# A graph-attention layer on one core: GpSimd normalises all four blocks of a group with the mean itself, and the steps around the first pass are reordered

## What is computed

```python
h = jnp.maximum(_layernorm(x, axis=-1), 0.0)      # mean and variance per row, eps 1e-5
Wh = h @ W
f1, f2 = Wh @ a[:128, 0], Wh @ a[128:, 0]
e = leaky_relu(f1[:, None] + f2[None, :], 0.2)
e = where(adj == 0, -inf, e)
out = x + softmax(e, axis=1) @ Wh
```

## Time and profile before

| | us |
|---|---|
| median of 3 runs | 812.27 |
| the runs | 810.42, 812.27, 812.67 |
| the profiled execution, its own time | 809.52 |
| its span in the trace | 807.8 |
| PE busy | 784.1 |
| DVE busy | 740.3 |
| ACT busy | 482.0 |
| POOL busy | 421.6 |

### The profile page before, as it was taken

The page is one execution under the profiler, slowest core; times in us unless marked ns, Lnnn a source line. Parts: engine busy times, 40 slices in busy tenths (PEclk is TensorE's granted clock), DMA queues, the critical chain, the costliest instruction groups (busy, mean ns, idle before and its releaser), DMA issues.

```text
span 807.8 us, 22596 instructions
## 1 busy us (share of the span) xinstructions
PE 784.1 (97%) x8971; PEld 718.4 (89%) x8971; DVE 740.3 (92%) x1191; ACT 482.0 (60%) x776; POOL 421.6 (52%) x621
## 2 busy tenths in 40 slices
PE   5789999999999999999999999999999999999997
PEld 4679899999999999999999999999999999999986
DVE  7898899999999999999999999999999999999996
ACT  5688855655655555565555556565555656555542
POOL 8778755544545454454545445554544545454320
PEclk9999999999999999999999999999999999999999
DMA  9999899999999999999999999999999999998200
GB/s 180 165 106 88 79 108 117 108 93 110 85 101 91 101 90 89 110 85 101 89 103 90 88 109 87 100 87 105 90 88 105 90 101 86 106 89 88 27 14 17
DMA packets 48069, 75.99 MB, mean 94 GB/s; under 512 B 4514, under 2 KB 13348, under 8 KB 48036
## 3 DMA queue, kind: packets, MB, share of 16 engines
q0 software_dynamic: 43008, 67.13, 88.4%
q1 hardware_dynamic: 4880, 8.39, 3.0%
q10 hardware_dynamic: 148, 0.07, 0.0%
HBM read 272.70 MB, written 4.19 MB: 343 GB/s over the span
## 4 chain that ended last, share of the span: by engine, by line
PE 91%; DMA 4%; DVE 3%; issue 1%; ACT 1%; POOL 0%; ACTq 0%; DVEq 0%; POOLq 0%
PE acc L404 54%; PE acc L408 28%; PE stage L394 7%; DMA masks<-in_adj_dram 2%; DVE wt_ring L847 2%; DMA xm<-in_x_dram 2%; PE stage L377 1%; PE stage L386 1%; PE stage L359 0%; DVE pairs L837 0%; POOL masks L225 0%; DVE stats L778 0%; ACT marks L598 0%; DVE xm L949 0%; ACT xn L548 0%
## 5 line engine op out<-in xcount | busy, mean ns | idle before, releaser
L847 DVE SCALAR_TENSOR_TENSOR wt_ring<-stage,packed,marks 128x512 f32<-128x512 f32 x1024 | 697.7, 744 | 52.3 <-PE acc L408 42.4
L404 PE MATMUL acc<-pairs,wt_ring 128*128 128x258 f16 x4096 | 719.8, 274 | 4.0 <-DVE pairs L837 2.8
L408 PE MATMUL acc<-pairs,wt_ring 128*128 128x129 f16 x4096 | 698.1, 219 | 0.0
L404 PEld LDWEIGHTS acc<-pairs,wt_ring 128*128 128x128 f16 x4096 | 396.2, 97 | 59.1 <-DVE pairs L837 4.5
L598 ACT ACTIVATE marks<-stage 128x1024 uint16<-128x1024 uint8 x256 | 262.1, 1024 | 290.2 <-PE stage L394 289.4
L408 PEld LDWEIGHTS acc<-pairs,wt_ring 128*128 128x128 f16 x4096 | 399.7, 98 | 2.5
L246 POOL TENSOR_TENSOR masks<-masks 128x256 int32<-128x256 int32 x256 | 184.4, 735 | 238.1 <-ACT masks L618 237.3
L219 POOL DMA_DIRECT2D masks<-in_adj_dram x240 | 130.3, 545 | 99.5 <-PE stage L394 77.4
L618 ACT ACTIVATE masks<-masks 128x512 uint16<-128x512 uint16 x256 | 158.9, 622 | 2.7 <-DMA masks<-in_adj_dram 2.7
L394 PE MATMUL stage<-ident,masks 128*128 128x128 f32 x512 | 98.9, 275 | 0.7 <-ACT marks L598 0.5
L394 PEld LDWEIGHTS stage<-ident,masks 128*128 128x128 f32 x512 | 53.0, 141 | 5.3 <-issue 1.7
(11 more groups left out here) (67 smaller groups left out, 144.5 us busy)
## 6 DMA issues: line engine op xcount, KB each, us to landing
masks<-in_adj_dram POOLq DMA_DIRECT2D x256, 256.0 KB, 7.3
out_dram<-xm SPq DMA_DIRECT2D x15, 256.0 KB, 7.2
xm<-in_x_dram SPq DMA_DIRECT2D x1, 1536.0 KB, 13.2
xm<-in_x_dram SPq DMA_DIRECT2D x2, 512.0 KB, 5.7
xm<-in_x_dram SPq DMA_DIRECT2D x1, 1024.0 KB, 10.1
xm<-in_x_dram SPq DMA_DIRECT2D x2, 256.0 KB, 3.0
out_dram<-xm SPq DMA_DIRECT2D x4, 64.0 KB, 2.3
wx<-in_L_gnn_W_dram ACTq DMA_DIRECT2D x1, 64.0 KB, 3.1
```

The lines of the kernel that those rows point to most:

```text
L404: return nc.tensor.matmul(acc[:, r, 0:2 * E1], wtv[:, w, r, 1, :], pairv[:, t, :, 0:E1], start=st, stop=end)
L408: return nc.tensor.matmul(acc[:, r, 0:E1], wtv[:, w, r, 0, :], pairv[:, t, 0, 0:E1], start=False, stop=False)
L847: nc.vector.scalar_tensor_tensor(out=wtq[:, t % NW], in0=e_row, scalar=packed[:, t, 1:2], in1=edges[:, k], op0=ALU.max, op1=ALU.mult).then ...
```

## The change

1. Normalising: ACT's block goes to POOL, which now does all four, as (x - mean) * rstd from `stats` and `small`. The offset, its instruction on DVE, and ACT's normalise are gone.
2. Variance: ACT's `root` takes the variance from `stats` with scale 1/D and bias eps, so DVE's instruction that adds eps no longer lies ahead of it and stands inside `inverses`.
3. Order: DVE's `inverses` for the batches 6-9 and 10-15 stand between the second and the third weight block of a unit, not behind statistics. On POOL `normalise` stands ahead of `scaled` in every b, and `normalise(3)` ahead of `mix(1)`. On ACT `root` stands ahead of `second` for these batches, and in b = 0 one `second` goes to the end. On PE the mask transposes of unit 1 move from ahead of the loop to behind two of the four steps of unit 0, and `features(2)` and `x_transposes(3)` with them.
4. Later masks: two blocks come in one transfer (`load_half`), so half as many transfers are issued.

```diff
-    SECONDS = {0: (2, 3), 13: (16,), 14: (17, 18), 15: (19, 20, 21)}
+    SECONDS = {0: (2,), 13: (16,), 14: (17, 18), 15: (19, 20, 21)}
     MIXES = {13: (15, 16), 14: (17, 18), 15: (19,)}
     PARTS = {0: (12,), 1: (13,), 2: (14, 15)}
     FIRSTS = {3: 4, 6: 5, 10: 6, 14: 7}
@@ -119,9 +118,9 @@
...
-                pool.wait_ge(s["ln_ready"], batch_of(g))
+                pool.wait_ge(s["ln_ready"], batch_of(g) + 1)
                 pool.wait_ge(s["xt_ready"], g - 1)
-                for r in range(1, PACK):
+                for r in range(PACK):
                     t = g * PACK + r
                     ins = nc.gpsimd.tensor_scalar(xn[:, g % 2, r * P:(r + 1) * P], xm[:, g, r * P:(r + 1) * P],
-                                                  small[:, 5, t:t + 1], small[:, 6, t:t + 1], ALU.mult, ALU.add)
+                                                  stats[:, t, 1:2], small[:, 5, t:t + 1], ALU.subtract, ALU.mult)
                 ins.then_inc(s["xn_pool"], 1)
...
+            def load_half(q, c, h):
+                at = c * PACK + HALF * h
+                nc.gpsimd.dma_start(masks[:, at:at + HALF, :], adj_half[q, c, :, HALF * h:HALF * (h + 1), :]
+                                    ).then_inc(adj_second[c] if h else adj_loaded[c], 16)
...
                 pool.wait_ge(s["mixed"], (n - NC + 1) * KC)
-                for r in (2, 3):
-                    load(n // NC, n % NC, r)
+                load_half(n // NC, n % NC, 1)
...
                 pool.wait_ge(s["transposed"], (n - NC + 1) * KC)
-                for r in (0, 1):
-                    load(n // NC, n % NC, r)
+                load_half(n // NC, n % NC, 0)
...
             mix(0)
             scaled(0)
             normalise(2)
+            normalise(3)
             mix(1)
-            normalise(3)
             scaled(1)
             load_part(EARLY)
             load_part(EARLY + 1)
             for b in range(UN):
                 for u in MIXES.get(b, (b + 2,)):
                     mix(u)
-
-                if b + 4 < NQ and b not in ROOTS:
+                if b + 4 < NQ:
                     normalise(b + 4)
                 if b + 2 < NQ:
                     scaled(b + 2)
-                if b + 4 < NQ and b in ROOTS:
-                    normalise(b + 4)
                 for u in PARTS.get(b, ()):
                     load_part(u)
...
-            pe.wait_ge(s["marked"], 1)
-            transposes(1, 1)
...
+                    if b == 0 and k == 1:
+                        pe.wait_ge(s["marked"], 1)
+                        transposes(1, 1)
+                    if b + 2 < NQ and k == (1 if b == 0 else 0):
                         features(b + 2, 0)
-                    if b + 3 < NQ and k == 0:
-                        x_transposes(b + 3)
-                    if b + 2 < NQ and k == 1:
+                        if b + 3 < NQ:
+                            x_transposes(b + 3)
+                    if b + 2 < NQ and k == (2 if b == 0 else 1):
                         features(b + 2, 1)
...
-                nc.scalar.activation(small[:, 4, sl], small[:, 1, sl], ACT.Ln).then_inc(s["log_ready"], 1)
+                if k == 0:
+                    act.wait_ge(s["cst_ready"], 3)
+                if k == 0:
+                    act.wait_ge(s["mean_ready"], CENTRED)
+                else:
+                    act.wait_ge(s["var_ready"], k)
+                nc.scalar.activation(small[:, 4, sl], stats[:, sl, 2], ACT.Ln, scale=1.0 / D, bias=cst[:, 2:3]
+                                     ).then_inc(s["log_ready"], 1)
...
             root(1)
             unpack(0, 0, first=True)
             high_part(0)
-            second(0, 1)
-            normalise(2)
             keep_scaled(0)
             keep_scaled(1)
             exponentials(1)
+            second(0, 1)
             relu(2)
             unpack(1, 1, first=True)
-            normalise(3)
...
+                if b in ROOTS and b > 0:
+                    root(ROOTS[b])
                 for u in SECONDS.get(b, (b + 3,)):
                     second(u // UN, u % UN)
-                if b in ROOTS:
+                if b == 0:
                     root(ROOTS[b])
                 if b + 3 < NQ:
                     relu(b + 3)
@@ -698,8 +698,8 @@
                     exponentials(b + 2)
                 if b + 2 < UN:
                     unpack(b + 2, b + 2, first=True)
-                if b + 4 < NQ:
-                    normalise(b + 4)
+                if b == 0:
+                    second(0, 3)
...
-                if g < CENTRED or any(hi == g + 1 for lo, hi in BATCHES):
-                    then(ins)
-
-            def moments(k):
+                if g < CENTRED:
+                    ins.then_inc(s["mean_ready"], 1)
+                elif any(hi == g + 1 for lo, hi in BATCHES):
+                    ins.then_inc(s["var_ready"], 1)
+            def inverses(k):
 
                 sl = slice(BATCHES[k][0] * PACK, BATCHES[k][1] * PACK)
-                both = small[:, 1, sl]
-                nc.vector.tensor_scalar(both, stats[:, sl, 2], 1.0 / D, EPS, ALU.mult, ALU.add
-                                        ).then_inc(s["var_ready"], 1)
-
-            def inverses(k):
-
-                sl = slice(BATCHES[k][0] * PACK, BATCHES[k][1] * PACK)
-                both, root, square, rstd, shift = (small[:, n, sl] for n in (1, 3, 4, 5, 6))
+                both, root, square, rstd = (small[:, n, sl] for n in (1, 3, 4, 5))
+                if k == 0:
+                    dve.wait_ge(s["mean_ready"], CENTRED)
+                else:
+                    dve.wait_ge(s["var_ready"], k)
+                nc.vector.tensor_scalar(both, stats[:, sl, 2], 1.0 / D, EPS, ALU.mult, ALU.add)
                 dve.wait_ge(s["root_ready"], k + 1)
                 then(nc.vector.tensor_tensor(square, root, root, ALU.mult))
                 then(nc.vector.scalar_tensor_tensor(out=square, in0=square, scalar=-0.5, in1=both,
                                                     op0=ALU.mult, op1=ALU.mult))
-                then(nc.vector.scalar_tensor_tensor(out=rstd, in0=square, scalar=1.5, in1=root,
-                                                    op0=ALU.add, op1=ALU.mult))
-                if BATCHES[k][1] <= CENTRED:
-                    return
-                nc.vector.scalar_tensor_tensor(out=shift, in0=stats[:, sl, 1], scalar=-1.0, in1=rstd,
-                                               op0=ALU.mult, op1=ALU.mult).then_inc(s["ln_ready"], 1)
+                nc.vector.scalar_tensor_tensor(out=rstd, in0=square, scalar=1.5, in1=root,
+                                               op0=ALU.add, op1=ALU.mult).then_inc(s["ln_ready"], 1)
...
-                weights(1, b, range(0, HALF if b == 0 else PACK))
-                low_part(b)
+                weights(1, b, range(0, HALF))
                 if b == 0:
-                    weights(1, b, range(HALF, PACK))
+                    low_part(b)
+                elif b - 1 in ROOTS and b > 1:
+                    inverses(ROOTS[b - 1])
+                weights(1, b, range(HALF, PACK))
+                if b > 0:
+                    low_part(b)
...
             nc.vector.tensor_scalar(wx[:, E1:WC], stage[:, 1, 1:2], -1.0, None, ALU.mult).then_inc(s["wx_ready"], 1)
             statistics(1)
-            moments(0)
             centre(1)
             inverses(0)
             statistics(2)
             keep_scaled(0)
             keep_scaled(1)
             statistics(3)
-            moments(1)
             pack(0)
             inverses(1)
             first_weights(0)
             pack(1)
             statistics(4)
             statistics(5)
-            moments(2)
...
-                if b in ROOTS and b > 0:
-                    inverses(ROOTS[b])
-                if b in LAST:
-                    moments(LAST[b])
```

More of the change, by code:

```diff
@@ L158, in gat_kernel @@
         adj_dram = adj.rearrange("(q p s) (c k) -> q s c p k", p=P, s=PACK, k=CHUNK)
+        adj_half = adj.rearrange("(q p s) (c k) -> q c p s k", p=P, s=PACK, k=CHUNK)
         adj_first = adj.rearrange("(q p s) (b k) -> q b p s k", p=P, s=PACK, k=BANK)
@@ L541, in _ @@
         def _(act):
-            def normalise(g):
-                act.wait_ge(s["ln_ready"], batch_of(g))
-                act.wait_ge(s["xt_ready"], g - 1)
-                t = g * PACK
-                nc.scalar.activation(xn[:, g % 2, 0:P], xm[:, g, 0:P], ACT.Identity, scale=small[:, 5, t:t + 1],
-                                     bias=small[:, 6, t:t + 1]).then_inc(s["xn_ready"], 1)
             def relu(g):
@@ L567, in keep_scaled @@
             def keep_scaled(h):
+                act.wait_ge(s["ln_ready"], 1)
                 act.wait_ge(s["whp_ready"], 2 + h + 1)
@@ L814, in keep_scaled @@
             def keep_scaled(h):
+                dve.wait_ge(s["ln_ready"], 1)
                 dve.wait_ge(s["whp_ready"], h + 1)
```

20 lines of the change are left out of this document (9 added, 11 removed).

## The result

The changed kernel takes 824.88 us, the median of 4 runs (824.65 to 825.14); the kernel before, in 4 runs beside it, took 811.35 (809.80 to 812.67). The ratio is 1.0174, with a 95% interval of 1.0157 to 1.0191: slower by some 14 us, where I had forecast 3.3 us faster and a range that ended at 812.3. The profiled execution took 824.98 us, its span is 823.2.

What follows compares the result with a forecast made beforehand. DVE's list was taken as the bound from 30 to 57 us, PE afterwards. Successive earlier starts bring unit 8 forward 3.6 us, less 0.3 for the lock: 3.3 us, 812.27 to 809.0; range 805.5 to 812.3 (own range 807.3 to 809.9).

Steps and rivals of the forecast that it cites:

- Eight blocks on POOL: POOL's normalising of groups 2 and 3: 0.43 to 0.50 us a block; DVE starts unit 1 at 18.4, 0.6 us earlier.
- POOL's pace: POOL's list for one b: 4.1 to 4.6 us against PE's 4.5; fused transfers save 0.5 us in eight b.
- rival 3: Lock and POOL's list eat the gain: five low_part hit as at 55.38 lose 2.5 us; 811.5, no change; chance 0.28.
- Start: First-pass start: pack(0) and root no longer wait for the eps addition; unit 0's weights start at 12.6 for 13.53, 0.9 us.
- Unit 1 and 2: Earlier normalise(4), but later scaled(2): most of PE's 1.33 us wait comes back; unit 3's weights start 0.55 us earlier.
- Inverses in the middle: DVE in unit 3: ln_ready earlier, PE's 2.08 us wait goes; unit 4 starts 0.4 us earlier, unit 5 2.5 us.
- Units 5 to 8: DVE at 4.86 us a unit; PE starts unit 8 at 59.0 for 62.6, 3.6 us earlier.
- the half clock: PE's 3.4 us at half clock from about 38 us, costing 1.7 us; forecast gone, clock 1.00 all through the first pass.
- Lock: DVE's low_part and POOL's SBUF reading exclude each other in units 3 to 7; 0.3 us taken off the gain.
- Rival 4: Slower fused transfer bounds every unit from 95 us on; at 20% slower costs 17 us, 826; chance 0.06.
- Rival 5: New start: mix(1) behind eight blocks, unit 1 late by 2.5 us through locks, nothing comes back; 815; chance 0.04.

Runs made afterwards that it cites:

- the last version: Kernel before with inverses in the middle and fused transfers, plus POOL normalising ahead of scaling in b = 0, 2, 6 and ACT's second of part 3 last: 805.49 us.
- the order with three blocks: Changed kernel's order, variance and fused transfers, but three blocks on POOL as multiply and add and one on ACT: 808.08 us, ratio 0.9972 to the kernel before.
- add and multiply with the old start: Changed kernel with add-multiply for subtract-multiply, four blocks on POOL, mix(1) between the two groups and unit 1's mask transposes ahead of the loop: 807.88 us, ratio 0.9971.

## Why the prediction was wrong

That the kernel became slower, and not faster, comes from one term. The step that failed is *Eight blocks on POOL*: "A block costs 1.30 / 3 = 0.43 us where nothing is in its way; the mean of 42 is 0.50". Those rows are of multiply and add. The change also exchanges the operations, and I carried the price over without a word, though subtract and multiply stood nowhere in the trace. 0.43 to 0.50 was the spread of the old form, no bound for the new one. A block measured 0.79 alone and 0.82 in the kernel.

*POOL's pace* took its four blocks from there, 1.73 to 2.0 us. They take 3.14, which brings the sum of 4.1 to 4.6 us for a unit to 5.5 to 5.7, over PE's 4.5. The round of 6.15 has 0.5 us more than that, most of it in a mask addition of 1.22 for 0.75; the mean round is 6.00. This crossing turns a price into time: below it a longer list on POOL fills gaps, above it nearly all goes to the end. I had the crossing as rival 3, but only with the lock to push it, and gave it nothing beyond a lost gain.

The other steps, as far as the runs show them:
- *Start* (0.9 us): in the changed kernel's profile the weights of unit 0 start at 14.18, later than the 13.53 before, but there the first masks came 1.6 us late. In four profiles of versions with ACT's new variance whose masks were on time they start at 12.84 to 13.00, so 0.5 to 0.7 of the 0.9 us are there. No time came of it where this part alone was added to another version: the lead was gone at 24 us.
- *Unit 1 and 2*: `mix(1)` behind eight blocks made unit 1 late by 3.5 us instead of early by 0.6. 2.4 of that are the same wrong price and 1.0 the late masks. At the cheap price, with masks on time, unit 1 starts at 18.99, so the 0.6 us of this step weren't there either. Its other claim, that the wait of 1.33 us comes back for the most part, was right as far as the last version shows: 0.38 and 0.61 us of waits are left in its place, and by the ratios 0.5 us of time came of it, with overlapping intervals.
- *Inverses in the middle* and *Units 5 to 8*: the gain that I forecast for all, 3.3 us, is about what this part alone brings (3.1 by the ratio). That agreement is partly luck, since in that run the half clock is at another place rather than gone. The whole change at the cheap price of the blocks brought 0.5 us with the offset (ratio 0.9994) and 2.1 with the negated mean (0.9974).
- *Lock* (0.3 us off): right in kind. The Trainium skill ("SBUF — State Buffer", Who interferes with whom) says that a DVE instruction with two SBUF inputs and GpSimd's reading keep each other out for their whole length; this case's trace agrees, with 1.49 us for a `low_part` of 0.68 beside a scaling of 1.05. The 2.11 us are more than one scaling of 1.04 explains. Its size I can't give: one hit cost up to 1.43 us instead of the 0.83 I allowed, but how much of that reaches the end no run separates. Rival 3 also took 0.5 us for a hit "as at 55.38", where that row has 0.83, so its five hits would have been 4.2 us and not 2.5.
- The price of a transfer of two blocks, taken as 0.65 us, measured 0.73.
- Rival 4 gave 826, near the 824.88 measured, by a mechanism that isn't there: the steady part is as before, and the fused transfers alone are a microsecond faster. Rival 5 had the right place in unit 1 but one place only, and laid it to locks and not to the price; POOL's pace from group 4 on was the larger part, 12.3 us of the 14.1 by which group 15 is late.

## What to carry to other kernels

Before a price is taken from a row, compare the operations and not only the opcode and the shape: the profile's row has the same name, TENSOR_SCALAR, for 447 and for 792 ns. When work is moved to an engine, add up that engine's list for one round and set it against the round of the bound; a term that is small against the span (16 us of 810) can be more than a quarter of a round (1.1 to 1.4 of 4.5 us). Before a step is judged by one profile, look at when the transfers that it waits for came in. And (x - mean) * r can be had at the cheap price, by adding the negated mean, which costs one instruction on a small tile for a batch.

## What the runs showed of the hardware that was not expected

- On POOL, a tensor_scalar on 128 x 128 f32 takes 447 ns for multiply-add, add-multiply and multiply-multiply with operands from SBUF, and 792 to 793 ns for subtract-multiply, multiply-subtract and add-add. One operation alone, subtract or multiply, takes 602, more than a cheap pair of two. The kernel before has such a row itself, the multiply alone at 128 x 516 (L281, 1525 ns, 15 times); whether a second operation would make that one cheaper wasn't run.
- At 128 x 512 the two kinds take 767 and 2072 ns, subtract alone 1562. From the two sizes, a further column costs (767 - 447) / 384 = 0.83 ns in the cheap form and (2072 - 792) / 384 = 3.33 in the dear one, four times as much, over much the same fixed part (340 and 365 ns). With immediate operands the two forms take 298 and 643 at 128 x 128.
- PE fell to half clock behind a wait of 1.33 us in some versions (granted clock 0.66 in 25 to 30 us with the inverses alone, and with the fused transfers alone) and not in the kernel before, where the wait was as long (1.00). What decides it isn't settled here.
- The first part of the masks comes early in some executions and late in others, with nothing in the kernels that explains it: ACT's first `second` starts between 9.03 and 9.47 us in nine of the profiled executions and between 10.12 and 10.99 in four (the changed kernel, the order with three blocks, the fused transfers, and add and multiply with the old start). What it costs in time isn't shown, since only one execution of each kernel has a profile.
